# First batch of a cross-attention kernel: TensorE's transposes of the probabilities in 64-row halves, and part of a V group moved in front of them

## The chip, the cores and the metric

One Trainium2 chip, one of its cores. The metric is the device time of one execution in microseconds (us), taken as the median of several runs; a profiled execution gives the trace beside it.

## What is computed

Shapes: `x` (as `x1`) and `ctx_2048` (as `x2`) are 8 x 512 x 1024, `Wq` and `Wk` 64 x 512, `Wv` 512 x 512, all float32. Cut to what matters:

```python
q = jnp.einsum('bcn,dc->bnd', x1, Wq) + bq
k = jnp.einsum('bcn,dc->bdn', x2, Wk) + bk[:, None]
v = jnp.einsum('bcn,dc->bdn', x2, Wv) + bv[:, None]
attn = jax.nn.softmax(jnp.einsum('bnd,bdm->bnm', q, k), axis=2)
attn_out = jnp.einsum('bcm,bnm->bcn', v, attn)
return attn_out + x1
```

## The kernel before

Every engine has its program written out by hand, and semaphores connect them. A batch has 1024 rows of scores in eight tiles of 128 rows (`ST` = 8), four for each half of the output columns. For precision each operand of a product is split into a rounded part and a rest (`_hi`, `_lo`), and a product is three matmuls in fp32r. From the second batch on, and in the first from its second half on, most matmuls run as pairs: 64 rows of the contraction on the upper row side of TensorE's array and 64 on the lower, into different PSUM banks; a second pass, with the sides exchanged, adds what is missing (`swap`). PSUM is `acc_ps` (four banks, for V, q and the output) and `s_ps` (two slots of two banks, for scores and k).

The probabilities must stand transposed as an operand of the output product. Later tiles are transposed by VectorE in 32x32 blocks and put in place by DMAs. The first four tiles of the first batch are done by TensorE itself: `first_turn(t)` issues eight transposes of 128x128 (float32, the identity as the moving operand) out of `probs0`, a view of the tile `blocks`, into two PSUM banks: `acc_ps` banks 2 and 3 for t of 0 and 1, `s_ps` slot 0 for t of 2, slot 1 for t of 3 (`t_banks`). The last of the eight raises `s_blk`.

The order around that, in the main program of TensorE (L1462 to L1475): scores of tiles 2 and 3; transposes of tile 0; `first_v_group(6)`, one of eight groups of V with 12 matmuls of 512 columns; transposes of tiles 1, 2, 3; `first_v_group(7)`; then `scores_rows(4)`, six half-row matmuls into `s_ps` slot 0, and `scores_rows(5)` into slot 1; then the loop body `batch(0)`. The waits there:

```python
first_turn(3)
first_v_group(7)
pe.wait_ge(s_qdup_b, 2)
pe.wait_ge(s_plo, 2)
scores_rows(4)
pe.wait_ge(s_plo_odd, 2)
scores_rows(5)
```

`s_norm` counts normalised tiles (VectorE for tiles 0, 2 and 3, ScalarE for tile 1). `s_qsum` says that VectorE has read the q sum out of `acc_ps` bank 3. After `s_blk`, ScalarE copies the transposed tile t out of PSUM (`first_p_hi(t)`, `pt_hi`, L488), and VectorE then forms the rest out of the same banks (`first_p_lo(t)`, `pt_lo`, L751). That rest raises `s_plo` for t of 0 and 2 and `s_plo_odd` for t of 1 and 3. ScalarE's order is `first_p_hi(0)`, exponentials of tiles 2 and 3, `first_q_high_b`, `first_p_hi(1)`, `(2)`, `(3)`, then V groups 6 and 7; VectorE's is `first_p_lo(0)`, `first_normalise(2)` and `(3)`, `first_q_low_b`, `first_p_lo(1)`, `(2)`, `(3)`, then the maxima of tiles 4 and 5.

Of the kernel before, what the change touches and what calls it, by code (L numbers as in the profile page):

```python
# [41 lines left out]
B, C, N, D = 8, 512, 1024, 64  # L42
P = 128
KT = C // P
CT = C // P
MT = N // P
HALVES = 2
NH = N // HALVES
NT = NH // P
# [3 lines left out]
BANKS = 4  # L53
# [24 lines left out]
def build(nc, x1_d, x2_d, bq_d, bk_d, bv_d, front_d, out_d):  # L78
# [3 lines left out]
    with ExitStack() as ctx:  # L82
        def sb(name, shape, dt):
            return ctx.enter_context(nc.sbuf_tensor(name, shape, dt))
# [4 lines left out]
        def sem(name):  # L89
            return ctx.enter_context(nc.semaphore(name))  # L90
# [25 lines left out]
        ident = sb("ident", [P, P], F32)  # L116
# [17 lines left out]
        probs0 = blocks[:].rearrange("p j m t r -> p (j m t r)").rearrange("p (t n) -> p t n", t=NT)  # L134
# [57 lines left out]
        s_qsum = sem("s_qsum")  # L192
# [11 lines left out]
        s_inv = sem("s_inv")  # L204
        s_norm = sem("s_norm")
        s_blk = sem("s_blk")
        s_phi = sem("s_phi")
        s_plo = sem("s_plo")
        s_plo_odd = sem("s_plo_odd")
# [5 lines left out]
        s_acc = sem("s_acc")  # L215
# [17 lines left out]
        def t_banks(t):  # L233

            return acc_ps[:, 2:4, :] if t < 2 else s_ps[:, t % 2, :, :]
# [852 lines left out]
        def _(pe):  # L1088
# [248 lines left out]
                v_second(nb, 4)  # L1337
                v_second(nb, 6)

            def first_turn(t):  # L1340
                pe.wait_ge(s_norm, t + 1)
                if t == 0:
                    pe.wait_ge(s_acc, BANKS + 4)
                    pe.wait_ge(s_qsum, 1)
                elif t == 1:
                    pe.wait_ge(s_plo, 1)
                for m in range(MT):
                    mm = nc.tensor.transpose(t_banks(t)[:, m // NT, (m % NT) * P:(m % NT + 1) * P],  # L1348
                                             probs0[:, t, m * P:(m + 1) * P], ident[:])
                mm.then_inc(s_blk, 1)  # L1350

            def first_k(k, h):
                for part, x in enumerate((xs_hi, xs_lo)):
# [19 lines left out]
            def first_v_group(m, ks=range(KT)):  # L1373
                if ks[0] == 0:
                    pe.wait_ge(s_acc, BANKS + (1, 2, 5, 6)[m - 4])
                for k in ks:
                    for x, w in ((xs_hi, wv_hi), (xs_hi, wv_lo), (xs_lo, wv_hi)):
                        mm = nc.tensor.matmul(acc_ps[:, V_BANK0[m], :], x[:, k, m * P:(m + 1) * P], w[:, k, :],  # L1378
                                              start=(k == 0 and x is xs_hi and w is wv_hi),
                                              stop=(k == KT - 1 and x is xs_lo))  # L1380
                if ks[-1] == KT - 1:
                    mm.then_inc(s_v, 1)
# [79 lines left out]
            scores_next(0, 2)  # L1462
            scores_next(0, 3)
            pe.wait_ge(s_ident, 1)
            first_turn(0)
            first_v_group(6)
            first_turn(1)
            first_turn(2)
            first_turn(3)
            first_v_group(7)  # L1470
            pe.wait_ge(s_qdup_b, 2)
            pe.wait_ge(s_plo, 2)
            scores_rows(4)
# [42 lines left out]
```

## Time and profile before

| what | value |
|---|---|
| median of 3 runs | 634.64 us (634.5 to 635.55) |
| the profiled execution's own time | 634.51 us |
| its span, first to last instruction | 632.7 us |
| TensorE (PE) busy | 629.1 us, 99% of the span, 5318 matmuls |
| VectorE (DVE) busy | 457.3 us, 72% |
| ScalarE (ACT) busy | 328.1 us, 52% |
| GpSimd (POOL) busy | 236.5 us, 37% |
| DMA | 94.18 MB, mean 149 GB/s |
| granted TensorE clock, mean | 1.000 |

How to read it: a matmul's recorded duration is longer than the distance to the next one, because matmuls are pipelined and their ends are modelled. So what a matmul takes from TensorE is read from the starts. Recorded durations of the other engines end where the result is there.

### The profile page before, as it was taken

Reading aid. Unit: us, or ns where it says so; the run is one execution under the profiler, and the core shown is the slowest. Engines: PE = TensorE matmul, PEld = TensorE weight load, DVE = VectorE, ACT = ScalarE, POOL = GpSimd, SP = SyncE. Lnnn points to the kernel's source line nnn. Section 1 sums busy time; section 2 is a strip of 40 time slices with the busy share of each in tenths; the row PEclk is TensorE's granted clock in tenths of the full one; section 3 lists DMA queues with packets and bytes.
Section 4 is the critical chain, followed back from the end, with each engine's and each line's share of the span. In section 5 each row is a group of like instructions: output and inputs, shape, how many; then the busy total and the mean of one; then the engine's idle time right before and its main releaser. Section 6 shows DMA issues by size and latency. Waiting matters only on the chain.

```text
span 632.7 us, 13476 instructions
## 1 busy us (share of the span) xinstructions
PE 629.1 (99%) x5318; PEld 523.0 (83%) x5318; DVE 457.3 (72%) x511; ACT 328.1 (52%) x430; POOL 236.5 (37%) x175
## 2 busy tenths in 40 slices
PE   9999999999999999999999999999999999999998
PEld 7888888888888888888888888888888888888886
DVE  6995778858788587885778857888568786597351
ACT  6786635735457345565455553554626547265120
POOL 0336204671047700487005860068501683026300
PEclk9999999999999999999999999999999999999999
DMA  8533326843267432755328542285323952343432
GB/s 342 203 138 77 115 74 181 304 101 112 73 183 283 100 130 84 196 235 133 99 83 233 221 125 88 104 263 189 103 93 116 271 186 80 99 133 99 101 125 76
DMA packets 39878, 94.18 MB, mean 149 GB/s; under 512 B 7216, under 2 KB 9264, under 8 KB 39856
## 3 DMA queue, kind: packets, MB, share of 16 engines
q1 hardware_dynamic: 39856, 93.88, 47.6%
q8 instruction: 15, 0.25, 0.2%
q14 instruction: 7, 0.06, 0.0%
HBM read 51.64 MB, written 16.78 MB: 108 GB/s over the span
## 4 chain that ended last, share of the span: by engine, by line
PE 99%; DMA 1%; DVE 0%; issue 0%
PE acc_ps L1183 52%; PE acc_ps L1140 23%; PE s_ps L1105 6%; PE s_ps L1253 4%; PE s_ps L1240 4%; PE acc_ps L1203 3%; PE acc_ps L1378 2%; PE acc_ps L1363 1%; PE acc_ps L1215 1%; PE s_ps L1354 1%; DMA pt_raw<-in_front_dram 1%; PE acc_ps L1369 0%; PE acc_ps L1348 0%; PE s_ps L1097 0%; PE s_ps L1098 0%; PE acc_ps L1386 0%
## 5 line engine op out<-in xcount | busy, mean ns | idle before, releaser
L1183 PE MATMUL acc_ps<-pt_hi,vt_lo 64*128 64x512 f32 x960 | 186.9, 386 | 0.0
L1183 PE MATMUL acc_ps<-pt_hi,vt_hi 64*128 64x512 f32 x960 | 186.9, 386 | 0.0
L1183 PE MATMUL acc_ps<-pt_lo,vt_hi 64*128 64x512 f32 x960 | 186.8, 386 | 0.0
L432 POOL TENSOR_TENSOR pt_raw<-blocks,const-float32-0.0 32x1024 f32<-32x1024 f32 x15 | 33.1, 2203 | 252.2 <-DVE blocks L870 245.8
L1183 PEld LDWEIGHTS acc_ps<-pt_lo,vt_hi 64*128 64x128 f32 x960 | 90.0, 184 | 18.9
L1183 PEld LDWEIGHTS acc_ps<-pt_hi,vt_lo 64*128 64x128 f32 x960 | 89.9, 184 | 18.8
L1183 PEld LDWEIGHTS acc_ps<-pt_hi,vt_hi 64*128 64x128 f32 x960 | 89.9, 184 | 18.8
L581 ACT ACTIVATE probs<-s_ps,negmax 128x1024 f32<-128x1024 f32 x56 | 62.6, 1118 | 54.8 <-DVE negmax L838 54.3
L838 DVE TENSOR_REDUCE negmax<-s_ps 128x1 f32<-128x1024 f32 x64 | 76.7, 1210 | 19.7 <-PE s_ps L1107 18.9
L1140 PE MATMUL acc_ps<-wv_lo,xs_hi 64*128 64x512 f32 x448 | 88.1, 390 | 0.0
L1140 PE MATMUL acc_ps<-wv_hi,xs_hi 64*128 64x512 f32 x448 | 87.2, 386 | 0.0
L1140 PE MATMUL acc_ps<-wv_hi,xs_lo 64*128 64x448 f32 x448 | 81.4, 360 | 0.0
L386 POOL TENSOR_TENSOR xs_lo<-stage,xs_hi 128x1024 fp32r<-128x1024 f32 x29 | 71.9, 2500 | 22.4 <-ACT xs_hi L488 22.0
L890 DVE SCALAR_TENSOR_TENSOR o_sb<-acc_ps,bias_v,o_sb 128x512 f32<-128x512 f32 x64 | 45.0, 741 | 43.2 <-PE acc_ps L1183 28.3
L488 ACT ACTIVATE pt_hi<-pt_raw 128x1024 fp32r<-128x1024 f32 x60 | 61.2, 1059 | 22.4 <-PE acc_ps L1183 21.8
L870 DVE STREAM_TRANSPOSE blocks<-probs 128x1024 f32<-128x1024 f32 x56 | 69.4, 1240 | 2.0
L488 ACT ACTIVATE vt_hi<-acc_ps 128x512 fp32r<-128x512 f32 x64 | 35.3, 596 | 56.0 <-PE acc_ps L1140 54.3
L751 DVE TENSOR_TENSOR vt_lo<-acc_ps,vt_hi 128x512 fp32r<-128x512 f32 x64 | 41.4, 686 | 31.5 <-ACT vt_hi L488 31.5
L488 ACT ACTIVATE xs_hi<-stage 128x1024 fp32r<-128x1024 f32 (+1 forms) x60 | 57.9, 1026 | 0.9 <-DMA stage<-in_front_dram 0.6
L436 POOL COPY pt_raw<-blocks 32x1024 f32<-32x1024 f32 x45 | 56.9, 1265 | 2.6
L751 DVE TENSOR_TENSOR xs_lo<-stage,xs_hi 128x1024 fp32r<-128x1024 f32 (+1 forms) x31 | 56.0, 1825 | 1.1 <-ACT xs_hi L488 1.1
L751 DVE TENSOR_TENSOR pt_lo<-pt_raw,pt_hi 128x1024 fp32r<-128x1024 f32 x46 | 53.9, 1208 | 1.4 <-ACT pt_hi L488 1.3
(142 smaller groups left out, 929.0 us busy)
## 6 DMA issues: line engine op xcount, KB each, us to landing
pt_raw<-blocks SPq DMA_DIRECT2D x180, 128.0 KB, 2.3
stage<-in_x_dram SPq DMA_DIRECT2D x32, 512.0 KB, 5.9
o_sb<-in_x_dram SPq DMA_DIRECT2D x64, 256.0 KB, 3.0
out_dram<-o_sb SPq DMA_DIRECT2D x63, 256.0 KB, 2.1
stage<-in_ctx_dram SPq DMA_DIRECT2D x28, 512.0 KB, 8.6
pt_raw<-in_front_dram SPq DMA_DIRECT2D x4, 512.0 KB, 5.7
v_part<-sums SPq DMA_DIRECT2D x56, 32.0 KB, 1.8
stage<-in_front_dram SPq DMA_DIRECT2D x2, 512.0 KB, 7.5
```

The lines of the kernel that those rows point to most:

```text
L386: return nc.gpsimd.tensor_tensor(out, src, hi.bitcast(F32), ALU.subtract)
L432: nc.gpsimd.tensor_tensor(pt_raw[0:Q, 0, :, :], first, nc.const_aps.tensor_like(0.0, first), ALU.add).then_inc(s_stay, 1)
L436: nc.gpsimd.tensor_copy(pt_raw[rows, j, :, :], blocks[rows, j, :, :, :].rearrange("p m t r -> p m (t r)")).then_inc(s_stay, 1)
L488: return nc.scalar.activation(out, in_, ACT.Copy)
L581: nc.scalar.activation(probs[:, t % 2, :], s_ps[:, t % 2, :, :].rearrange("p a n -> p (a n)"), ACT.Exp, bias=negmax[:, t:t + 1], accum_out ...
L751: return nc.vector.tensor_tensor(out, a, hi.bitcast(F32), ALU.subtract)
L838: nc.vector.tensor_reduce(negmax[:, t:t + 1], s_ps[:, t % 2, :, :].rearrange("p a n -> p (a n)"), AX_X, ALU.max, negate=True).then_inc(s_m ...
L870: nc.vector.transpose(turned_blocks(i), probs[:, t % 2, :].rearrange("p (m j r) -> p m j r", j=NQ, r=Q)).then_inc(s_blk, 1)
L890: nc.vector.scalar_tensor_tensor(out=o_sb[:, c, :], in0=acc_ps[:, OUT_BANK[c], :], scalar=bias_v[:, c:c + 1], in1=o_sb[:, c, :], op0=ALU.a ...
L1105: nc.tensor.matmul(s_ps[:, t % 2, 0, :], q_top[0:D, rows], k[0:D, 0:NH], start=(q_top is q_st and k is k_hh), stop=(k is k_ll))
L1140: mm = nc.tensor.matmul(acc_ps[:, V_BANK[tile], 0:width], x[rows, k, tile * P:(tile + 1) * P], w[rows, k, 0:width], start=(swap == 0 and k ...
L1183: mm = nc.tensor.matmul(acc_ps[:, OUT_BANK[group], :], v[rows, m, group * P:(group + 1) * P], p[rows, m, :], start=(swap == 0 and m == 0 a ...
```

## The change

`first_turn` gets a second argument. Each 128x128 transpose becomes parts that read 64 rows and write 64 columns. For swap 0, the upper 64 rows go into the first of the tile's two banks while the lower 64 rows go into the second, in four pairs; for swap 1 the sides exchange banks. The second pass waits until the first is complete, through a new semaphore `s_turn_rows`, so that the two row sides never write to the same bank. So a tile has 16 transposes of 64 rows instead of 8 of 128. For tile 0 the two passes stand one behind the other. For tiles 1 to 3 the passes are interleaved. And the first six matmuls of V's group 7 (its first two of four slices of the contraction) now stand behind group 6, ahead of tile 1, the other six behind tile 3.

```diff
+        s_turn_rows = sem("s_turn_rows")
...
-            def first_turn(t):
-                pe.wait_ge(s_norm, t + 1)
-                if t == 0:
-                    pe.wait_ge(s_acc, BANKS + 4)
-                    pe.wait_ge(s_qsum, 1)
-                elif t == 1:
-                    pe.wait_ge(s_plo, 1)
-                for m in range(MT):
-                    mm = nc.tensor.transpose(t_banks(t)[:, m // NT, (m % NT) * P:(m % NT + 1) * P],
-                                             probs0[:, t, m * P:(m + 1) * P], ident[:])
-                mm.then_inc(s_blk, 1)
+            def first_turn(t, swap):
+
+                if swap == 0:
+                    pe.wait_ge(s_norm, t + 1)
+                    if t == 0:
+                        pe.wait_ge(s_acc, BANKS + 4)
+                        pe.wait_ge(s_qsum, 1)
+                    elif t == 1:
+                        pe.wait_ge(s_plo, 1)
+                else:
+                    pe.wait_ge(s_turn_rows, t + 1)
+                for j in range(NT):
+                    for side in range(2):
+                        rows, a = slice(side * D, side * D + D), (side + swap) % 2
+                        m = a * NT + j
+                        mm = nc.tensor.transpose(t_banks(t)[:, a, j * P + side * D:j * P + side * D + D],
+                                                 probs0[rows, t, m * P:(m + 1) * P], ident[rows, rows])
+                mm.then_inc(s_blk if swap else s_turn_rows, 1)
...
-            first_turn(0)
+            first_turn(0, 0)
+            first_turn(0, 1)
             first_v_group(6)
-            first_turn(1)
-            first_turn(2)
-            first_turn(3)
-            first_v_group(7)
+            first_v_group(7, range(0, 2))
+            first_turn(1, 0)
+            first_turn(2, 0)
+            first_turn(1, 1)
+            first_turn(3, 0)
+            first_turn(2, 1)
+            first_turn(3, 1)
+            first_v_group(7, range(2, KT))
```

TensorE's order from the last matmul of V's group 6 to the scores of tile 4, before (names are destination, moving operand, stationary operand; in brackets the semaphores waited for; an `x7` stands for seven alike):

```order
L1378 MATMUL acc_ps<-wv_hi,xs_lo 128x512
L1348 MATMUL acc_ps<-ident,blocks 128x128 [waits s_plo,s_norm]
L1348 MATMUL acc_ps<-ident,blocks 128x128 x7
L1348 MATMUL s_ps<-ident,blocks 128x128 [waits s_norm]
L1348 MATMUL s_ps<-ident,blocks 128x128 x7
L1348 MATMUL s_ps<-ident,blocks 128x128 [waits s_norm]
L1348 MATMUL s_ps<-ident,blocks 128x128 x7
L1378 MATMUL acc_ps<-wv_hi,xs_hi 128x512 [waits s_acc]
```

And the same place in the change; ahead of these rows stand the six matmuls of group 7 that moved, behind them its other six:

```order
L1356 MATMUL acc_ps<-ident,blocks 128x64 [waits s_plo,s_norm]
L1356 MATMUL acc_ps<-ident,blocks 128x64 x7
L1356 MATMUL s_ps<-ident,blocks 128x64 [waits s_norm]
L1356 MATMUL s_ps<-ident,blocks 128x64 x7
L1356 MATMUL acc_ps<-ident,blocks 128x64 [waits s_turn_rows]
L1356 MATMUL acc_ps<-ident,blocks 128x64 x7
L1356 MATMUL s_ps<-ident,blocks 128x64 [waits s_norm]
L1356 MATMUL s_ps<-ident,blocks 128x64 x7
L1356 MATMUL s_ps<-ident,blocks 128x64 [waits s_turn_rows]
L1356 MATMUL s_ps<-ident,blocks 128x64 x7
L1356 MATMUL s_ps<-ident,blocks 128x64 [waits s_turn_rows]
L1356 MATMUL s_ps<-ident,blocks 128x64 x7
```

What moved: tile 1, which was complete after the first eight transposes behind group 6, is now complete after six V matmuls and 24 half transposes. Tile 0 changes in the same way in place:

```order
L1356 MATMUL acc_ps<-ident,blocks 128x64 [waits s_acc,s_qsum,s_norm,s_ident]
L1356 MATMUL acc_ps<-ident,blocks 128x64 x7
L1356 MATMUL acc_ps<-ident,blocks 128x64 [waits s_turn_rows]
L1356 MATMUL acc_ps<-ident,blocks 128x64 x7
L1386 MATMUL acc_ps<-wv_hi,xs_hi 128x512 [waits s_acc]
```

Its second pass is directly behind its first, with nothing between. The orders of the other engines stay as they were.

## Rows read from the trace of the kernel before

**Rows 1.** The page: busy time of each engine, and its chain that ended last.

```profile
PE 629.1 (99%) x5318; PEld 523.0 (83%) x5318; DVE 457.3 (72%) x511; ACT 328.1 (52%) x430; POOL 236.5 (37%) x175
...
PE 99%; DMA 1%; DVE 0%; issue 0%
```

**Rows 2.** The waits of TensorE, whole span: total us, times, longest us.

```profile
PE s_ps L1403 <- PEq L1491: 0.8, 1, 0.8
```

**Rows 3.** Timeline of TensorE at tile 0: start, us, what, count.

```profile
32.36 0.39 PE L1098 MATMUL s_ps<-k_ll,q_st 128*128 128x512 f32 x1
32.70 1.06 PE L1348 MATMUL acc_ps<-ident,blocks 128*128 128x128 f32 x8
...
33.84 0.39 PE L1378 MATMUL acc_ps<-wv_lo,xs_hi 128*128 128x512 f32 x1
```

**Rows 4.** Timeline of TensorE at tiles 1 to 3.

```profile
36.13 0.39 PE L1378 MATMUL acc_ps<-wv_hi,xs_lo 128*128 128x512 f32 x1
36.36 1.05 PE L1348 MATMUL acc_ps<-ident,blocks 128*128 128x128 f32 x8
...
39.23 0.39 PE L1378 MATMUL acc_ps<-wv_lo,xs_hi 128*128 128x512 f32 x1
```

**Rows 5.** Timeline of TensorE from V's last matmul to the scores of tiles 4 and 5.

```profile
41.52 0.39 PE L1378 MATMUL acc_ps<-wv_hi,xs_lo 128*128 128x512 f32 x1
...
42.17 0.39 PE L1105 MATMUL s_ps<-k_hh,q_dup 64*128 64x512 f32 x1
42.18 0.39 PE L1107 MATMUL s_ps<-k_hh,q_st 64*128 64x512 f32 x1
...
42.64 0.39 PE L1105 MATMUL s_ps<-k_hh,q_st 64*128 64x512 f32 x1
```

**Rows 6.** Timeline of TensorE in batch 7, from half-row pairs to full rows.

```profile
604.86 0.39 PE L1183 MATMUL acc_ps<-pt_hi,vt_lo 64*128 64x512 f32 x2
...
607.58 0.39 PE L1183 MATMUL acc_ps<-pt_hi,vt_lo 64*128 64x512 f32 x2
...
608.23 0.40 PE L1203 MATMUL acc_ps<-pt_lo,vt_hi 128*128 128x512 f32 x1
```

**Rows 7.** Timeline of TensorE in batch 1: half-row pairs of 448 and 512 columns.

```profile
99.78 0.37 PE L1140 MATMUL acc_ps<-wv_hi,xs_lo 64*128 64x448 f32 x2
99.98 0.39 PE L1140 MATMUL acc_ps<-wv_lo,xs_hi 64*128 64x512 f32 x2
```

**Rows 8.** Groups of weight loads by form, 30 to 40 us: busy us, mean ns.

```profile
L1348 PEld LDWEIGHTS s_ps<-ident,blocks 128*128 128x128 f32 x16 | 1.8, 140 | 0.0
...
L1097 PEld LDWEIGHTS s_ps<-k_hh,q_st 128*128 128x128 f32 x4 | 0.8, 188 | 0.2
```

**Rows 9.** Groups of TensorE's transposes by form: busy us, mean ns.

```profile
L1348 PE MATMUL s_ps<-ident,blocks 128*128 128x128 f32 x16 | 1.9, 272 | 0.0
```

**Rows 10.** Timeline of ScalarE: its copies of tiles 0, 1, and 2 with 3.

```profile
33.80 1.03 ACT L488 ACTIVATE pt_hi<-acc_ps 128x1024 fp32r<-128x1024 f32 x1 [0.92 <-PE acc_ps L1348]
...
37.45 1.03 ACT L488 ACTIVATE pt_hi<-acc_ps 128x1024 fp32r<-128x1024 f32 x1
38.37 1.94 ACT L488 ACTIVATE pt_hi<-s_ps 128x1024 fp32r<-128x1024 f32 x2
```

**Rows 11.** Timeline of VectorE: q sum, tiles' rests, normalising of tile 3.

```profile
31.81 0.74 DVE L765 SCALAR_TENSOR_TENSOR sums<-acc_ps,bias_q,sums 64x512 f32<-64x512 f32 x1 [0.43 <-ACT sums L488]
...
34.97 1.23 DVE L751 TENSOR_TENSOR pt_lo<-acc_ps,pt_hi 128x1024 fp32r<-128x1024 f32 x1
...
37.25 0.75 DVE L855 TENSOR_SCALAR blocks<-blocks,inv 128x1024 f32<-128x1024 f32 x1
38.03 0.69 DVE L751 TENSOR_TENSOR q_st<-sums,q_st 64x512 fp32r<-64x512 f32 x1
38.75 1.22 DVE L751 TENSOR_TENSOR pt_lo<-acc_ps,pt_hi 128x1024 fp32r<-128x1024 f32 x1
39.89 2.35 DVE L751 TENSOR_TENSOR pt_lo<-s_ps,pt_hi 128x1024 fp32r<-128x1024 f32 x2
```

## The prediction

> **What bounds the kernel now.** First the page's busy times and its chain that ended last: TensorE is busy 99% of the span, and 99% of the chain is its own work [rows 1]. Then the waits of TensorE: the only one in 632.7 us is at the start, 0.8 us [rows 2]. So whatever moves TensorE's program here moves the end by as much, and nothing behind the changed place (32 to 43 us) would take a delay back, since TensorE stands still nowhere there. A shorter stretch is worth what it saves only if no wait takes its place. That is to be read in three timelines: TensorE's, ScalarE's and VectorE's between 32 and 43 us.
>
> On TensorE the reader is to see the distances of starts. A matmul of 512 columns, or a pair of half-row ones, takes 0.227 us: between 604.86 and 607.58 lie twelve pairs, 2.72 us, and the ten V matmuls from 33.84 to 36.13 take 2.29 [rows 3, 4, 6]. Tile 0's eight transposes follow a matmul at 32.36, and the second V matmul behind them starts at 33.84, so the first really starts 0.227 earlier, at 33.61 [rows 3]. The 24 transposes of tiles 1 to 3 begin at 36.36, and by the same reckoning V goes on at 39.00: 2.64 us, 0.110 each [rows 4]. The scores of tile 4 have their second pair at 42.17, so their first at 41.94 [rows 5].
>
> On ScalarE and VectorE the reader is to see a chain that is nearly as long as TensorE's work. ScalarE's copy of tile 1 runs from 37.45 to 38.48 [rows 10]. VectorE, with a q rest from 38.03 to 38.72, begins tile 1's rest at 38.75, and then has 39.89 + 2.35 = 42.24 as the end of tile 3's [rows 11]. The scores of tile 5 must wait for exactly that; they start at 42.64 [rows 5]. From VectorE to TensorE a hand-off takes 0.15: the q sum ends at 31.81 + 0.74 = 32.55 and tile 0 starts at 32.70, where an unhindered TensorE would have started at 32.36 + 0.227 = 32.59 [rows 3, 11]. So the slack there is 42.64 - 42.39 = 0.25 us, and no more.
>
> **The parts and their costs.**
>
> *A pair of half transposes, p.* No row shows one. A 128-column transpose takes 0.110, and half the columns on both sides at once would take 0.055; half-row pairs do run side by side, since a pair of 512 columns takes what one full matmul takes, and its two starts lie 0.01 apart [rows 5, 6]. That is the lower bound. The upper one is 0.20, the shortest distance of pairs that the trace has (448 columns, 99.78 to 99.98), if issuing two loads and two matmuls sets the pace [rows 7]. I take 0.065, half of 0.110 plus that 0.01: what is nearest are the transposes themselves, and their weight loads are recorded at 140 ns where those of fp32r are 188, so the load has room to be hidden [rows 8]. The Trainium skill says otherwise (TensorE: Matmul & The Clock Gate, LDWEIGHTS): a load's time goes with its columns, about columns / 1.2 ns, and not with its rows. By that a pair would take about 0.107 and halving the rows would gain nothing; two loads one behind the other in 0.20 us [rows 7] already exclude 0.107 each in series, but not side by side.
>
> *Changing between full rows and half rows.* It costs 0.20 each time, both ways: 607.58 to 608.23 is 0.65 where two matmuls take 0.454, and 41.52 to 42.17 likewise [rows 5, 6]. The new kind starts 0.03 behind the recorded end of the last matmul. The change adds four: into and out of tile 0, into and out of tiles 1 to 3; the one before scores of tile 4 is there already.
>
> *The wait for the first pass.* A transpose of 128 columns ends 0.272 after its start [rows 9], 0.11 of it columns; so a half one ends after 0.22. Add 0.15 for the hand-off, the row from VectorE; the lower bound is 0.04, TensorE to ScalarE at tile 0 (last transpose starts 33.49, ends 33.76, ScalarE 33.80) [rows 3, 10].
>
> *Tile 0.* First pair 32.36 + 0.39 + 0.03 = 32.78 (32.70 before). First pass ends 3 x 0.065 + 0.22 later, 33.20; second pass starts 33.35 and ends 33.76, as before, so ScalarE and VectorE behind it see no difference. V starts 0.03 later, at 33.79 instead of 33.61: 0.18 lost. The empty pipeline between the passes eats what the halves save.
>
> *V's moved half.* 18 matmuls instead of 12 stand between tile 0 and tile 1. They cost TensorE nothing in total, but tile 1 starts at 33.79 + 17 x 0.227 + 0.39 + 0.03 = 38.07, against 36.36. Its other waits are long met: tile 0's rest ended at 36.20, and tile 3, the last, was normalised at 38.00 [rows 11].
>
> *Tiles 1 to 3.* First pass of tile 1 at 38.07, last pair 38.27, complete at 38.64 with the hand-off; tile 2's pass covers all but 0.05 of that. Tile 1 is complete at 38.64 + 0.195 + 0.22 = 39.05. With one more stall of 0.05 at the end V goes on at 39.91. That is 1.84 us for 24 pairs where 2.64 stood. The six V matmuls end so that tile 4's scores could start at 39.91 + 5 x 0.227 + 0.42 = 41.46, 0.48 before the 41.94 of now. Were TensorE alone, this 0.48 would be the gain.
>
> *What is late next.* ScalarE waits for tile 1, which was complete before it came to it. Now it copies at 39.09, done at 40.12, and VectorE begins tile 1's rest at 40.15 instead of 38.75: 1.40 later. The next two follow at the old distances, so tile 2's rest ends at about 42.47 and tile 3's at 43.64. TensorE, ready at 41.46, is held for tile 2 until 42.62 (1.16 us), runs three pairs, 0.69, and is held again from 43.31 to 43.79 for tile 3. The scores of tile 5 start at 43.79 instead of 42.64: **1.15 us later**, which is 1.40 less the slack of 0.25. SP's and GpSimd's queues have nothing to do with these steps, and no later wait is near enough to matter.
>
> The sum is 634.51 + 1.15 = 635.66 for the profiled execution's time. The median of the runs is 0.13 higher, so 635.79, which I give as 635.8. It is 0.18% slower. A measurement of this kernel can tell some 0.2% (1.27 us) from no change, so the forecast lies just inside that, and p at 0.075 instead of 0.065 (12 pairs stand ahead of the end of tile 1) brings it to 1.27.
>
> **The rivals.**
>
> *Slower: the load or the issue sets the pace.* With p = 0.11, what a full transpose takes now, tile 0 loses 0.27 more, tile 1 is complete 0.72 later than above, and TensorE goes on 1.87 later than before: 636.5. It decides from p = 0.075 on. For it: the full weights' 128 columns are still loaded for every half, so twice the loads. Against it: the shorter load rows. At p = 0.20 it would be 3.40 later, 638.0. The Trainium skill (same page, Wait — 56ns, not 53.3ns?) has 62 ns per matmul where firmware decodes; two of them would make 0.124 a pair, about 2.1 us later by the same sum.
>
> *The chain is shorter.* If changing kinds costs nothing for transposes (as into them at 36.36 now), the hand-off is 0.04 and p is 0.055, then V goes on behind tile 0 at about 33.4, tile 1 starts at 37.5, is complete at 38.35, and tile 5's scores start at about 43.1: 0.46 later, 635.1. For it: today's transposes are entered and left without loss [rows 4].
>
> *Faster: the chain does not decide.* If ScalarE and VectorE took tile 1 up no more than 0.25 later than now, only TensorE's own work would count. With my prices that is 0.48 less, 634.2. Only with the low prices, 24 x 0.055 = 1.32 and 0.45 at tile 0, would it reach 1.8 less, 632.9. Against it stands arithmetic: tile 1 is put behind six more V matmuls, 1.36 us, and VectorE's three rests of 1.17 each follow it in a row.
>
> *The change does not do what it says*: the halves do not run side by side. Then a pair takes 0.11 or more, which is the first rival.
>
> **How the numbers follow.** Forecast, p from 0.055 to 0.075 with four changes of kind: 0.42, of it 0.30 within 0.2% and 0.12 above. Slower rival around 0.11: 0.30. Beyond 0.15: 0.08, all slower. Shorter chain: 0.16, within 0.2%. Faster: 0.04. So faster 0.04, same 0.46, slower 0.50. The range begins at 635.0, just under the shorter chain's 635.1, and ends at 637.2, between the rival's 636.5 and the 638.0 that I leave out; outside are the 0.04, the 0.08 and some 0.08 of errors in the other cases.
>
> **What would show it.** In the changed kernel's timeline: pairs of half transposes 0.065 apart; a gap of some 0.3 us between the passes of tile 0; tile 1's copy on ScalarE near 39.1 and its rest on VectorE near 40.15; TensorE with two waits on VectorE's `pt_lo`, 1.16 and 0.48 us, the first it has behind the start; the scores of tile 5 at 43.8, and everything behind it moved by the same 1.15. I am wrong if tile 5's scores start before 43.0 or after 44.3, if TensorE shows no wait there, or if a later wait absorbs the shift.

## The result, and the profile after

The changed kernel takes 635.59 us (median of 22 runs, 635.02 to 636.8) against 634.65 (22 runs, 634.02 to 635.87): ratio 1.0015, 95% interval 1.0009 to 1.0022. That is 0.94 us more, where 1.15 was forecast. The interval leaves out 1, so the changed kernel is slower, though by less than the 0.2% that the prediction took as the bound of what can be told from no change. The profiled execution has a span of 633.4 us against 632.7.

These are the changed kernel's page, busy times and the chain that ended last, and behind them its waits of TensorE (total us, times, longest us):

```profile
PE 628.0 (99%) x5350; PEld 522.4 (82%) x5350; DVE 457.0 (72%) x511; ACT 328.1 (52%) x430; POOL 236.5 (37%) x175
...
PE 98%; DVE 1%; DMA 1%; ACT 0%; issue 0%
```

```profile
PE s_ps L1106 <- DVE pt_lo L752: 1.2, 1, 1.2
PE s_ps L1411 <- PEq L1504: 0.8, 1, 0.8
PE acc_ps L1371 <- DVE wv_hi L991: 0.6, 1, 0.6
```

TensorE is busy 1.1 us less, and yet the end is later: VectorE has appeared in the chain with 1%, and TensorE waits for its `pt_lo`, where [rows 1, 2] had nothing of the kind. The wait of 0.8 us was there before. The third lies at the start, in front of everything compared here.

The timelines have to be laid on each other first. The last score matmul ahead of tile 0 starts at 32.06, before at 32.36 [rows 3], since the first loads landed at other times. So 0.30 is to be added to the times of the changed kernel to read them on the clock of the kernel before. TensorE of the changed kernel (start, us, what, count):

```profile
32.06 0.39 PE L1099 MATMUL s_ps<-k_ll,q_st 128*128 128x512 f32 x1
32.40 0.99 PE L1356 MATMUL acc_ps<-ident,blocks 64*128 64x64 f32 x16
33.31 0.50 PE L1386 MATMUL acc_ps<-wv_hi,xs_hi 128*128 128x512 f32 x1
33.65 0.40 PE L1386 MATMUL acc_ps<-wv_lo,xs_hi 128*128 128x512 f32 x1
...
37.30 0.39 PE L1386 MATMUL acc_ps<-wv_hi,xs_lo 128*128 128x512 f32 x1
37.62 0.46 PE L1356 MATMUL acc_ps<-ident,blocks 64*128 64x64 f32 x8
37.91 0.42 PE L1356 MATMUL s_ps<-ident,blocks 64*128 64x64 f32 x8
38.17 0.44 PE L1356 MATMUL acc_ps<-ident,blocks 64*128 64x64 f32 x8
38.44 0.94 PE L1356 MATMUL s_ps<-ident,blocks 64*128 64x64 f32 x24
39.31 0.50 PE L1386 MATMUL acc_ps<-wv_hi,xs_hi 128*128 128x512 f32 x1
39.65 0.39 PE L1386 MATMUL acc_ps<-wv_lo,xs_hi 128*128 128x512 f32 x1
...
40.58 0.40 PE L1386 MATMUL acc_ps<-wv_hi,xs_lo 128*128 128x512 f32 x1
42.20 0.46 PE L1106 MATMUL s_ps<-k_hh,q_st 64*128 64x512 f32 x1 [1.23 <-DVE pt_lo L752]
...
43.24 0.49 PE L1106 MATMUL s_ps<-k_hh,q_st 64*128 64x512 f32 x1
...
44.04 0.39 PE L1184 MATMUL acc_ps<-pt_hi,vt_hi 64*128 64x512 f32 x2
```

At tile 0, V's second matmul starts 1.59 us behind the last scores (32.06 to 33.65), where it was 1.48 before [rows 3], so 0.11 is lost. At tiles 1 to 3, V's second matmul is at 39.65, 2.35 us behind V's last start at 37.30, with 24 pairs and both changes of kind in between. Before, that was 39.23 - 36.13 = 3.10 [rows 4], so 0.75 is saved. The last 24 half transposes, into `s_ps`, take 0.94 us together. A single one lasts 0.225, and the 11 distances between the twelve pairs share the rest, 0.065 each. The groups of transposes and of their weight loads between 30 and 46 us (busy us, mean ns):

```profile
L1356 PE MATMUL s_ps<-ident,blocks 64*128 64x64 f32 x32 | 1.4, 225 | 0.0
...
L1356 PEld LDWEIGHTS s_ps<-ident,blocks 64*128 64x128 f32 x32 | 1.2, 139 | 0.0
```

V's last matmul at 40.58 is at 40.88 on the clock of before, 0.64 ahead of the 41.52 there [rows 5], and 0.64 is also 0.75 less 0.11. All this is lost at 42.20, where TensorE stands still for 1.23 us.

The chain of the changed kernel in order of time (start, us, what) shows which engines hold it:

```profile
38.33 0.29 PE acc_ps L1356 x8
38.62 0.02 issue
38.64 1.03 ACT pt_hi L489
39.67 0.02 issue
39.70 3.50 DVE pt_lo L752 x3
43.20 0.04 issue
43.24 0.49 PE s_ps L1106
```

ScalarE copies tile 1 as soon as its second pass ends, and VectorE's three rests follow in one piece of 3.50 us, up to the scores of tile 5. The same in ScalarE's and VectorE's timelines, which answer to [rows 10, 11]:

```profile
38.64 1.02 ACT L489 ACTIVATE pt_hi<-acc_ps 128x1024 fp32r<-128x1024 f32 x1 [1.50 <-PE acc_ps L1356]
```

```profile
37.66 0.69 DVE L752 TENSOR_TENSOR q_st<-sums,q_st 64x512 fp32r<-64x512 f32 x1
39.70 1.23 DVE L752 TENSOR_TENSOR pt_lo<-acc_ps,pt_hi 128x1024 fp32r<-128x1024 f32 x1 [1.36 <-ACT pt_hi L489]
40.84 2.35 DVE L752 TENSOR_TENSOR pt_lo<-s_ps,pt_hi 128x1024 fp32r<-128x1024 f32 x2
```

Both engines now stand idle ahead of tile 1, by 1.50 and 1.36 us; before, both went from one piece of work to the next. The rest of tile 1 starts at 39.70 + 0.30 = 40.00 instead of 38.75, 1.25 later.

### The profile page after: what moved, and what is told of

Same layout as the page of the kernel before. It is cut to its first block, busy times and chain, and to the rows that moved or that the text cites. A ratio compares the mean times of both kernels' runs of the same rounds, so it can differ in the third digit from the quotient of the medians.

```text
span 633.4 us, 13540 instructions
## 1 busy us (share of the span) xinstructions
PE 628.0 (99%) x5350; PEld 522.4 (82%) x5350; DVE 457.0 (72%) x511; ACT 328.1 (52%) x430; POOL 236.5 (37%) x175
## 4 chain that ended last, share of the span: by engine, by line
PE 98%; DVE 1%; DMA 1%; ACT 0%; issue 0%
PE acc_ps L1184 52%; PE acc_ps L1141 23%; PE s_ps L1106 6%; PE s_ps L1241 4%; PE s_ps L1254 4%; PE acc_ps L1204 3%; PE acc_ps L1386 2%; PE acc_ps L1371 1%; PE acc_ps L1216 1%; PE s_ps L1362 1%; DVE pt_lo L752 1%; DMA pt_raw<-in_front_dram 1%; PE acc_ps L1377 0%; PE s_ps L1098 0%; PE s_ps L1099 0%; PE s_ps L1394 0%
```

## The experiments

Each time is beside runs of the kernel before on the same chip. In the timelines I take the distance from the last score matmul ahead of tile 0 to the first matmul of the loop body: 43.33 - 32.36 = 10.97 us before, read from its timeline, and 44.04 - 32.06 = 11.98 in the changed kernel. This distance is free of the start's variation. A second trace of the changed kernel, the last experiment below, gives 43.94 - 31.95 = 11.99, so it resolves some hundredths; the medians resolve some tenths. Of the 27 runs of the kernel before that stand beside the first four experiments, one took 3643.83 us, which does not move the median.

**The halves alone.**

```diff
-            first_v_group(7, range(0, 2))
...
-            first_v_group(7, range(2, KT))
+            first_v_group(7)
```

> The changed kernel with V's group 7 back in one piece behind tile 3: the halves alone. Chain theory (the time is set by when tile 1 is complete, and by ScalarE's and VectorE's copies behind it): in the changed kernel ScalarE's copy of tile 1 started 0.92 us behind the tile's first pair (37.72 and 38.64); without six V matmuls, 1.36 us, it can start at 37.28 on that profile's clock, 0.13 later than before, and VectorE is not late. Tile 3's first pass then meets the wait for its normalising (VectorE done at 37.62, so 37.77), which eats what the halves save. Sum: before + 0.1 us, between -0.2 and +0.3. TensorE shows no wait on pt_lo. Rival (the halves, their changes of kind and their hand-offs cost TensorE itself 1 us, and the wait only shows it elsewhere): before + 0.9 as in the changed kernel.

In this kernel V's group 7 stands in one piece behind tile 3 again.

Measured: 634.37 us against 634.46, ratio 1.0 (0.9991 to 1.001). The distance is 43.23 - 32.25 = 10.98, so before + 0.01. Its TensorE, from its timeline:

```profile
36.45 0.46 PE L1356 MATMUL acc_ps<-ident,blocks 64*128 64x64 f32 x8
37.00 0.46 PE L1356 MATMUL s_ps<-ident,blocks 64*128 64x64 f32 x8
37.30 0.41 PE L1356 MATMUL acc_ps<-ident,blocks 64*128 64x64 f32 x8
37.87 0.99 PE L1356 MATMUL s_ps<-ident,blocks 64*128 64x64 f32 x24 [0.16 <-DVE blocks L856]
```

No wait for `pt_lo`, as expected. Tiles 2 and 3 are held until VectorE has normalised them (37.00 where 36.45 + 4 x 0.065 = 36.71 was possible, and 37.87), and this takes what the halves save. The expectation was off in a detail: tile 2 waits too, so tile 1's second pass comes later and ScalarE takes tile 1 up at 37.75, not 0.13 but 0.41 later than before on the common clock. VectorE still was only 0.17 late, within its slack. The rival, that the halves themselves cost the microsecond, is out.

**The move alone.**

```diff
+            first_v_group(7, range(0, 2))
             first_turn(1)
             first_turn(2)
             first_turn(3)
-            first_v_group(7)
+            first_v_group(7, range(2, KT))
```

> The kernel before (transposes of 128 rows) with the first six matmuls of V's group 7 in front of tile 1: the move alone. Chain theory: tile 1 is complete 1.36 us later, ScalarE copies it 1.3 later, VectorE takes its rest up 1.1 later, less the slack of 0.25: before + 0.86 us, TensorE waits for pt_lo at the scores of tiles 4 and 5, 0.4 to 0.9 us in total. Rival (the halves cost it): before + 0.0, since the move adds nothing to TensorE.

Measured: 635.03 against 634.46, ratio 1.0013 (1.0004 to 1.0022). That is 0.57 us more, with an interval of some 0.25 to 1.4 us. The distance is 44.88 - 33.06 = 11.82: + 0.85. TensorE and VectorE of this kernel:

```profile
43.03 0.47 PE L1105 MATMUL s_ps<-k_hh,q_st 64*128 64x512 f32 x1 [0.48 <-DVE pt_lo L751]
```

```profile
40.53 1.23 DVE L751 TENSOR_TENSOR pt_lo<-acc_ps,pt_hi 128x1024 fp32r<-128x1024 f32 x1 [1.14 <-ACT pt_hi L488]
```

The transposes of before with nothing but the six V matmuls moved make 0.85 of the 1.01 us.

**Three V matmuls ahead instead of six.**

```diff
-            first_v_group(7, range(0, 2))
+            first_v_group(7, range(0, 1))
...
-            first_v_group(7, range(2, KT))
+            first_v_group(7, range(1, KT))
```

> The changed kernel with three V matmuls (one slice of four) in front of tile 1 instead of six. Chain theory: everything behind tile 1 is 0.68 us earlier than in the changed kernel, so before + 0.3 us (1.0 - 0.68), with a shorter wait on pt_lo. Rival: before + 0.9, as the changed kernel.

Measured: 634.34 against 634.46, ratio 1.0002 (0.9992 to 1.0011). The medians show nothing, the distance does: 44.06 - 32.76 = 11.30, + 0.33, with a wait on `pt_lo` of 0.5 us. So the timeline resolves 0.3 us and the runs don't.

**All twelve ahead.**

```diff
-            first_v_group(7, range(0, 2))
+            first_v_group(7)
...
-            first_v_group(7, range(2, KT))
```

> The changed kernel with all twelve matmuls of V's group 7 in front of tile 1. Chain theory: tile 1 complete another 1.36 us later, which nothing takes back: before + 2.3 us, and TensorE's wait on pt_lo at the scores of tile 4 grows from 1.2 to about 3.9 us, since V's six matmuls don't fill it any more. Rival (TensorE's own work decides): before + 0.9, the same as the changed kernel.

Measured: 638.39 against 634.46 (636.62 to 638.52 in five runs), ratio 1.0058 (1.0044 to 1.0071). The direction is the chain's, but 3.9 us is 1.6 more than expected, and the wait is 2.8 us, not 3.9: I had counted the moved matmuls twice, as a delay of tile 1 and as missing in front of the scores, though TensorE comes to the scores at nearly the same time as in the changed kernel (0.23 earlier). 1.23 + 1.36 + 0.23 is the 2.82 of the trace. The windows of its trace (us, length, busy of TensorE, weight loads, VectorE, ScalarE and GpSimd, granted clock, DMA share, GB/s) say where the rest went:

```profile
40.00:42.00 2.00, 0.96 (x30) 0.82 (x26) 0.72 (x1) 1.78 (x2) 0.00 (x0) 1.00 0.00 0
42.00:44.00 2.00, 0.22 (x2) 0.25 (x4) 2.00 (x3) 2.00 (x5) 0.00 (x0) 0.86 0.00 0
44.00:46.00 2.00, 2.00 (x10) 1.68 (x12) 1.30 (x2) 1.94 (x3) 0.86 (x1) 0.50 0.03 8
46.00:48.00 2.00, 2.00 (x16) 1.71 (x14) 1.95 (x3) 1.20 (x2) 2.00 (x2) 0.79 0.00 0
```

The granted clock falls to 0.50 (1.2 instead of 2.4 GHz) toward the end of a pause of 2.82 us, and the pairs of scores then lie 0.43 us apart. The window from 43.25 to 43.50 us has 0.88, the next quarter of a microsecond 0.50, and TensorE starts again at 43.78:

```profile
43.78 0.76 PE L1106 MATMUL s_ps<-k_hh,q_st 64*128 64x512 f32 x1 [2.82 <-DVE pt_lo L752]
...
45.20 0.62 PE L1106 MATMUL s_ps<-k_hh,q_st 64*128 64x512 f32 x1
45.23 0.63 PE L1108 MATMUL s_ps<-k_hh,q_dup 64*128 64x512 f32 x1
45.62 0.62 PE L1106 MATMUL s_ps<-k_hh,q_dup 64*128 64x512 f32 x1
```

**All twelve ahead, with the pause filled.** To see whether the clock makes the rest, four matmuls were added into the pause, into a PSUM bank that is free by then; nobody reads them:

```diff
+            pe.wait_ge(s_plo_odd, 1)
+            for i in range(4):
+                nc.tensor.matmul(acc_ps[:, 2, :], wv_hi[:, 0, 0:P], wv_hi[:, 0, :], start=True, stop=True)
             pe.wait_ge(s_qdup_b, 2)
             pe.wait_ge(s_plo, 2)
             scores_rows(4)
```

> The kernel with all twelve V matmuls ahead of tile 1 ran 3.9 us above before, where 2.3 were expected, and its profile has the granted clock at 0.5 from about 43.4 to 46.8 us, behind a pause of TensorE of 2.8 us. This one adds, as soon as VectorE is done with tile 1's rest, four matmuls of 512 columns that nobody reads, into the bank that is free by then, inside the pause. Clock theory: the pause is cut to about 1.7 us, the granted clock stays at 1.0, and the time falls, although work is added, to before + 2.3 us. Rival (the extra 1.6 us are not the clock's, but a longer chain): the time stays at before + 3.9 or rises.

Measured: 636.69 against 634.79, ratio 1.0032 (1.002 to 1.0044): + 1.9, so 1.7 us less than the same kernel without the added work beside it (638.41, the next experiment). The same windows:

```profile
42.00:44.00 2.00, 1.54 (x7) 1.02 (x9) 2.00 (x3) 2.00 (x5) 0.00 (x0) 1.00 0.00 0
44.00:46.00 2.00, 1.92 (x18) 1.27 (x16) 1.99 (x3) 1.90 (x3) 0.97 (x1) 1.00 0.03 8
```

```profile
42.45 1.21 PE L1485 MATMUL acc_ps<-wv_hi 128*128 128x512 f32 x4 [1.60 <-DVE pt_lo L752]
```

The pause is 1.60 us, and the clock stays. The distance is 45.51 - 32.16 = 13.35, + 2.38, as the chain theory had it; the medians, from six runs, say somewhat less.

**The same without the filling, beside it.**

> The kernel with all twelve V matmuls ahead of tile 1 once more, beside the one with the filled pause: before + 3.9 us and a granted clock of 0.5 behind the pause by the clock theory as by its rival. One of its five runs was 636.6 us, 2.2 above before: where the clock stays up in an execution, the time should be about that.

Measured: 638.41 (638.16 to 639.24) against 634.79, ratio 1.0063 (1.0049 to 1.0077), and again a clock of 0.50 behind a pause of 2.82 us. It fell later here, when the loop body had nearly begun: the window from 44 to 46 us has 0.80, that from 46 to 48 has 0.50. The pause ended at 43.53, and the first half microsecond below 1 is that from 45.00, with 0.71. All five runs have a mean granted clock below 1, 0.994 to 0.997. The first series had one short run, 636.62, and the mean granted clock tells it apart: it is 1.000 there and 0.997 in the four others. So the execution whose clock stayed up took before + 2.2, the chain's sum without the clock. No trace of it exists.

**The changed kernel with a short chain.** ScalarE's copies and VectorE's rests of tiles 1 to 3 leave out three quarters of the columns, where the output product then reads older values. TensorE's program is left alone.

```diff
+                few = slice(0, Q if t == 0 else Q // 4)
-                copy(pt_tile(pt_hi, t), turned(t)).then_inc(s_phi, 1)
+                copy(pt_tile(pt_hi, t)[:, few, :], turned(t)[:, few, :]).then_inc(s_phi, 1)
...
+                few = slice(0, Q if t == 0 else Q // 4)
-                sub(pt_tile(pt_lo, t), turned(t), pt_tile(pt_hi, t)).then_inc((s_plo, s_plo_odd)[t % 2], 1)
+                sub(pt_tile(pt_lo, t)[:, few, :], turned(t)[:, few, :],
+                    pt_tile(pt_hi, t)[:, few, :]).then_inc((s_plo, s_plo_odd)[t % 2], 1)
```

> The changed kernel, but ScalarE copies and VectorE subtracts only a quarter of the columns of tiles 1 to 3 (the other three quarters are left out and the output product reads older values there). Chain theory: with the chain short, the scores of tile 4 start as soon as TensorE is ready, at the end of V's last matmul plus 0.03: 40.58 + 0.39 + 0.03 = 41.00 on the changed profile's clock, where before has 41.94 - 0.30 = 41.64. So before - 0.6 us, and no wait on pt_lo: this is what the halves save on TensorE. Rival (the halves themselves cost 1 us): before + 0.9 still.

Measured: 633.85 against 634.35, ratio 0.9991 (0.9982 to 1.0); distance 42.30 - 31.97 = 10.33, - 0.64. TensorE and VectorE:

```profile
40.48 0.40 PE L1389 MATMUL acc_ps<-wv_hi,xs_lo 128*128 128x512 f32 x1
40.81 0.50 PE L1109 MATMUL s_ps<-k_hh,q_st 64*128 64x512 f32 x1
...
42.30 0.39 PE L1187 MATMUL acc_ps<-pt_hi,vt_hi 64*128 64x512 f32 x2
```

```profile
38.97 0.43 DVE L753 TENSOR_TENSOR pt_lo<-acc_ps,pt_hi 128x256 fp32r<-128x256 f32 x1 [0.72 <-ACT pt_hi L489]
39.48 0.76 DVE L753 TENSOR_TENSOR pt_lo<-s_ps,pt_hi 128x256 fp32r<-128x256 f32 x2
```

The same TensorE program now runs through. The scores of tile 4 follow V at the usual distance of a change of kind (0.33), and the 0.64 us that the halves save is there to be seen at the end.

**The kernel before with the short chain**, with the same edit and the same columns left out.

> The kernel before with the same three quarters of tiles 1 to 3 left out of ScalarE's copies and VectorE's rests. Chain theory: TensorE had 0.25 us of slack there and no wait, so the time stays: before + 0.0 us, within 0.2. If it becomes faster than before by over 0.3 us, the chain was already binding in a way that the timeline did not show, and the slack of 0.25 was misread.

Measured: 634.48 against 634.35, ratio 1.0003 (0.9994 to 1.0012); distance 42.99 - 32.04 = 10.95, - 0.02. So before, the chain held nothing back, and the short chain gains 1.65 us in the changed kernel (11.98 - 10.33) and nothing in the old one.

**The changed kernel once more.**

> The changed kernel once more beside it, on the same chip and with the same runs of before: before + 0.9 us, with the granted clock at 1.0 throughout, since its longest pause of TensorE is 1.2 us.

This is the changed kernel without any edit.

Measured: 635.29 against 634.66, ratio 1.0015 (1.0006 to 1.0024), and a distance of 11.99, with the clock at 1.00 in every window from 38 to 46 us.

## Why the prediction was right, and what in it was off

*Bound.* TensorE's program sets the end, and no later wait took anything back: the shift of 1.01 at the loop body less the 0.30 of the earlier start is the 0.7 by which the span grew.

*The pair.* 0.065 was taken and 0.065 measured. The slower rival, which rested on a pair of 0.11, is out, and so is the one at 0.20. That the value was hit exactly is partly luck, since the rows bounded it only by 0.055 and 0.20. By the rule of the Trainium skill (TensorE: Matmul & The Clock Gate, LDWEIGHTS) a load of 128 columns takes about 0.107 by estimate whatever its rows. As the pace of these transposes this does not hold, since two such loads are done in 0.065; that the rows don't matter agrees with the recorded duration of one load, 139 ns with 64 rows and 140 with 128 [rows 8]. Each half also has 64 moving columns instead of 128, and no run separates what sets the 0.065.

*Changes of kind.* The 0.20 for each was too much on the way into the transposes. From V's last start at 37.30 to V's second matmul at 39.65 lie 2.35 us; without changes there would be 24 x 0.065 + 2 x 0.227 = 2.01, so 0.34 for both and all hand-offs, where 0.48 was put (twice 0.20 and the stalls between passes). The first pass of tile 1 ends at 38.08, which reckoned back (0.225 and three distances of 0.065) puts its first pair at 37.66, 0.36 behind V's last start: so the way in costs 0.13. The way out costs about 0.20, as was put, and next to nothing is left for stalls.

*Hand-off between the passes.* The chain in order of time has it at tile 0:

```profile
32.45 0.42 PE acc_ps L1356 x8
32.87 0.04 issue
32.92 0.47 PE acc_ps L1356 x8
```

So it is 0.04 to the first load of the second pass, the lower bound. The 0.15 of the prediction counted up to where the matmul takes effect; reckoned back from the end of the second pass at 33.39 this is 32.97, 0.10 behind. With a slightly shorter way in, tile 0 lost 0.11 instead of 0.18.

*Tile 1's delay and what follows.* Its rest was forecast 1.40 late and is 1.25 late. Of these 0.15, tile 0 makes 0.07 and the way into tile 1's transposes 0.06. Less the slack of 0.25, 1.25 gives 1.00, and the distance says 1.01. The slack, the term that had only one pair of rows behind it, held, and not in this kernel alone. The rest of tile 1 starts, counted from the last scores ahead of tile 0 and beside the kernel before, 0.17 (the halves alone), 0.58 (three ahead), 1.08 (the move alone), 1.25 (the change) and 2.62 us (all ahead, filled) later; the loop body 0.01, 0.33, 0.85, 1.01 and 2.38 later. That is 0.25 less each time, within 0.02, and nothing where the delay is under 0.25. The move alone has 0.85 of the 1.01. The other 0.16 is tile 0's loss, the change of kind ahead of tile 1 and the two passes, less the shorter transposes.

*The waits.* 1.16 was forecast at tile 4 and 1.23 is shown. At tile 5, 0.48 was forecast. Its first pair is recorded 0.50 behind the last of tile 4, 42.74 to 43.24, where 0.23 would be usual, so 0.27. Reckoned back from its second pair (43.57 - 0.227 = 43.34) it is 0.36. On the clock of before that start is 43.64, where 43.79 was forecast and 42.64 was before.

*TensorE alone.* A gain of 0.48 was forecast for a kernel whose chain doesn't decide; the short chain shows 0.64, since the ways in and the hand-offs between passes cost less than was counted.

So the mechanism was right in each step. The forecast of 1.15 was 0.14 too much against the distance, and 0.21 against the medians, because the way into the transposes and the hand-off between the passes were priced from the nearest rows and cost less.

No version tried that does the whole work is faster than the kernel before. The saving of 0.64 us is real but out of reach while VectorE's chain has only 0.25 us of slack at the scores of tile 5. The halves alone met the normalising of tiles 2 and 3 as well; even without that wait, the slack would let through no more than a quarter of a microsecond (an estimate, not tested). Not tried was to take work off VectorE between 32 and 42 us.

## What to carry to other kernels

Work that is moved in front of a producer may save time on its own engine, but it delays whoever consumes what that producer makes: before moving it, follow the product through the engines behind it, and compare the delay with the slack at the place where the chain comes back. Two engines whose chain is nearly as long as the bounding engine's work let through no more than that slack, whatever is saved on the bounding engine. And a cut in work is shown best by cutting the chain around it for one experiment: it tells what the saving would be worth before one looks for a way to get it.

## What the runs showed of the hardware

In both traces of the kernel with all twelve ahead, a pause of TensorE of 2.82 us went with the lower granted clock (0.50) for between 3 and 3.5 us. In one trace the clock fell shortly before the pause ended, in the other about 1.7 us behind its end. It cost 1.6 to 1.7 us beside the pause, by the medians. Pauses of 1.60 and 1.23 us were not followed by it. Four matmuls whose result nobody reads, placed in the pause, made that kernel 1.7 us faster (638.41 to 636.69).

Float32 transposes of 64 rows by 64 columns ran as pairs on the two row sides at 0.065 us a pair, where one of 128 by 128 takes 0.110. The granted clock stayed at 1.00 through them. Going from full-row matmuls of 512 columns into them cost 0.13 us at tile 1, and back 0.20.
